# Masks of the attention maxima copied into PSUM by ScalarE instead of multiplied in by TensorE, with three rotating bank pairs and an earlier norm of the next input

## What is computed

```python
def xattn(query_in, ctx, mask, ...):            # both layers; mask and inner norms in the second only
    q = layernorm(query_in @ Wq + bq) ; k = layernorm(ctx @ Wk + bk) ; v = layernorm(ctx @ Wv + bv)
    scores = einsum('bhqd,bhkd->bhqk', heads(q), heads(k)) / sqrt(32)
    scores = where(mask == 0, -1e9, scores)      # mask: 2 x 2048 x 154, int32
    return merge(softmax(scores) @ heads(v)) @ Wo + bo
x = x + tanh(g_xattn[0]) * L0_xattn(layernorm(x), ctx)
x = x + tanh(g_ffn[0])   * L0_ffn(layernorm(x))          # 512 -> 2048 -> 512, relu
x = x + tanh(g_xattn[1]) * L1_xattn(ctx, layernorm(x), mask)
x = x + tanh(g_ffn[1])   * L1_ffn(layernorm(x))          # piecewise-linear gelu on a fixed-point grid
```

## Time and profile before

| | us |
|---|---|
| median of 3 runs | 2468.31 |
| lowest, highest | 2467.7, 2469.46 |
| the profiled execution | 2469.93 |
| its span in the profile | 2468.1 |
| TensorE busy | 2407.3 (98%) |
| TensorE weight loads busy | 1826.9 (74%) |
| VectorE busy | 1444.4 (59%) |
| ScalarE busy | 1086.7 (44%) |
| GpSimd busy | 244.6 (10%) |

### The profile page before, as it was taken

One profiled execution on the slowest core, in us unless ns is written; L12 is line 12 of the kernel. 1 busy time (PEld: TensorE's weight loads), 2 busy tenths in 40 slices (PEclk: granted clock), 3 DMA queues, 4 the chain that ended last, 5 costly groups with the idle time before them and its releaser, 6 DMA issues.

```text
span 2468.1 us, 33136 instructions
## 1 busy us (share of the span) xinstructions
PE 2407.3 (98%) x13344; PEld 1826.9 (74%) x13344; DVE 1444.4 (59%) x2410; ACT 1086.7 (44%) x1762; POOL 244.6 (10%) x223
## 2 busy tenths in 40 slices
PE   6999999999999999999989999999999999999998
PEld 5666667688888888888755666666778888888886
DVE  5555566542212222223566666665888888888986
ACT  4343433442222222223344333335566666666665
POOL 1011112210000000000311111113000000000000
PEclk9999999999999999999999999999999999999999
DMA  3121111421101101102311222223401101001000
GB/s 126 35 86 52 52 52 69 157 87 52 42 11 52 52 14 38 52 18 72 124 61 62 79 78 79 79 73 114 156 18 35 52 18 52 35 25 45 35 32 21
DMA packets 92600, 147.27 MB, mean 60 GB/s; under 512 B 5408, under 2 KB 28320, under 8 KB 92448
## 3 DMA queue, kind: packets, MB, share of 16 engines
q1 hardware_dynamic: 92448, 145.16, 17.6%
HBM read 111.59 MB, written 33.55 MB: 59 GB/s over the span
## 4 chain that ended last, share of the span: by engine, by line
PE 39%; DVE 9%; ACT 2%; issue 1%; DMA 0%; POOL 0%; SPq 0%; DVEq 0%; ACTq 0%
PE l_lay_bank L69 18%; PE l_lay_score L69 11%; PE l_lay_score L1416 1%; PE l_lay_score L1418 1%; PE l_lay_values L1494 1%; PE l_lay_sums L1506 1%; PE l_lay_values L1498 1%; DVE l_at_at_next L1036 1%; DVE l_at_h_lo L1050 1%; DVE l_at_at_next L1029 1%; PE l_lay_score L1477 1%; DVE l_at_full L1025 1%; DVE l_at_full L1018 1%; DVE l_at_xTf_lo L924 1%; DVE l_at_lay_stats L891 1%
## 5 line engine op out<-in xcount | busy, mean ns | idle before, releaser
L69 PE MATMUL l_lay_score<-l_at_tw_hi,l_at_h_hi 128*128 128x512 f32 x1024 | 401.5, 392 | 5.2 <-DVE l_at_h_lo L1050 4.7
L69 PE MATMUL l_lay_bank<-l_at_xTf_hi,l_at_tw_hi 128*128 128x512 f32 x1024 | 400.0, 391 | 0.0
L69 PE MATMUL l_lay_score<-l_at_tw_hi,l_at_h_lo 128*128 128x512 f32 x1024 | 398.7, 389 | 0.0
L69 PE MATMUL l_lay_score<-l_at_tw_lo,l_at_h_hi 128*128 128x512 f32 x1024 | 398.5, 389 | 0.0
L69 PE MATMUL l_lay_bank<-l_at_xTf_hi,l_at_tw_lo 128*128 128x512 f32 x1024 | 398.5, 389 | 0.0
L69 PE MATMUL l_lay_bank<-l_at_xTf_lo,l_at_tw_hi 128*128 128x512 f32 x1024 | 398.4, 389 | 0.0
L1010 DVE TENSOR_TENSOR l_at_h_lo<-l_at_full,l_at_h_hi 128x512 fp32r<-128x512 f32 x128 | 99.6, 779 | 465.9 <-ACT l_at_h_hi L740 465.9
L735 ACT ACTIVATE l_at_full<-l_lay_bank,l_at_lay_b 128x512 f32<-128x512 f32 x128 | 88.3, 690 | 457.6 <-PE l_lay_bank L69 457.6
L69 PEld LDWEIGHTS l_lay_score<-l_at_tw_hi,l_at_h_hi 128*128 128x128 f32 x1024 | 192.3, 188 | 49.2 <-DVE l_at_h_lo L1050 10.2
L69 PEld LDWEIGHTS l_lay_score<-l_at_tw_hi,l_at_h_lo 128*128 128x128 f32 x1024 | 192.2, 188 | 40.2
L69 PEld LDWEIGHTS l_lay_bank<-l_at_xTf_hi,l_at_tw_lo 128*128 128x128 f32 x1024 | 192.2, 188 | 40.0
(11 more groups left out here) (224 smaller groups left out, 4071.9 us busy)
## 6 DMA issues: line engine op xcount, KB each, us to landing
both_x_in<-stream SPq DMA_DIRECT2D x25, 1024.0 KB, 5.6
l_at_xg<-stream SPq DMA_DIRECT2D x23, 1024.0 KB, 5.6
stream<-l_at_xg SPq DMA_DIRECT2D x22, 1024.0 KB, 4.3
l_at_tw_raw<-in_l_w SPq DMA_DIRECT2D x64, 256.0 KB, 5.7
l_at_maskT_in<-in_maskT SPq DMA_DIRECT2D x40, 256.0 KB, 2.7
both_x_in<-in_x SPq DMA_DIRECT2D x9, 1024.0 KB, 7.6
l_at_xg<-in_x SPq DMA_DIRECT2D x7, 1024.0 KB, 5.4
out<-l_at_xg SPq DMA_DIRECT2D x7, 1024.0 KB, 4.3
```

Of the source, the lines that this page charges most:

```text
L69: done = nc.tensor.matmul(out, lhs[a], rhs[b], start=first and n == 0, stop=last and n == len(passes) - 1)
```

## The change

In the second layer, for chunks 1 to 7 and maxima 4 to 15, the mask is no longer multiplied in. ScalarE copies `mask_add` into the two banks (`seed_max`), and the key products accumulate onto it (start is false). The maxima 4 to 15 rotate over three bank pairs, the third being `values` and `sums`, now banks 4 and 5 of one tensor of six. A seed waits for the maximum three before it, seed 4 for the masks and for ScalarE's own copies of values and sums. TensorE waits for the seed instead of for the maximum two before. The high halves of query tiles 2 and 3 are made behind seeds 5 and 6. On VectorE, in the second layer, mask, first mask piece and the statistics of the next input stand behind the second query row, and its normalisation behind the third; GpSimd makes the input's scale before the queries' one.

```diff
-        score = n.ps("score", [P, GH, 512])
-        values = n.ps("values", [P, 512])
-        sums = n.ps("sums", [P, 512])
+        score = n.ps("score", [P, GH + 2, 512])
+        values, sums = score[:, GH, :], score[:, GH + 1, :]
...
+        SEED0 = 4
+        N_SEED = NM - SEED0
+        pair_of = lambda it, m: m % 2 if it == 0 or m < SEED0 else (m - 2) % 3
+        pair_before = lambda m: m - 3 if m > SEED0 else None
+        max_banks = lambda it, m: score[:, 2 * pair_of(it, m):2 * pair_of(it, m) + 2, 0:2 * KEYS]
...
+            def seed_max(it, m):
+                if m == SEED0:
+                    act.wait_ge(mask_done, it + 1)
+                    act.wait_ge(c_out, KT * it)
+                    act.wait_ge(s_out, it)
+                else:
+                    act.wait_ge(max_done, NM * it + pair_before(m) + 1)
+                nc.scalar.activation(max_banks(it, m).rearrange("p a (h k) -> p a h k", h=2),
+                                     mask_add[:, m % QT, :].unsqueeze(1).unsqueeze(1)
+                                     .broadcast_to([P, 2, 2, KEYS]), ACT.Copy).then_inc(seeded, 1)
...
                 c_evict(it, 3)
                 if more and norm:
-                    q_front_norm(it + 1, (2, 3))
+                    q_raw_norm(it + 1, 2)
+                    q_raw_norm(it + 1, 3)
                 s_evict(it)
+                if more and norm:
+                    for m in range(SEED0, NM):
+                        seed_max(it + 1, m)
+                        if m in (SEED0 + 1, SEED0 + 2):
+                            q_hi_norm(it + 1, m - SEED0 + 1)
...
+                    q_rows_front(it + 1, (0, 1))
+                    mask_front(it + 1)
+                    maskT_front(it + 1, 0)
+                    norm_stats(it + 2)
+                    q_rows_front(it + 1, (2,))
+                    norm_apply(it + 2)
+                    q_rows_front(it + 1, (3,))
                     q_norm_stats(it + 1)
+                    q_norm_apply(it + 1)
...
             def max_of(it, m):
                 t, q, b = m // QT, m % QT, it // CPB
+                seed = norm and it > 0 and m >= SEED0
...
-                if m >= 2:
+                if seed:
+                    pe.wait_ge(seeded, N_SEED * (it - 1) + m - SEED0 + 1)
+                elif m >= 2:
                     pe.wait_ge(max_done, NM * it + m - 1)
...
-                    if norm:
+                    if norm and not seed:
                         nc.tensor.matmul(to, ident_bf[:, :], mask_add[:, q, :].unsqueeze(1)
                                          .broadcast_to([P, 2, KEYS]), start=True, stop=False)
```

More of the change, by code:

```diff
@@ L590, in _ @@
                     add_bias(last, gate_bias)
+                if it < last:
+                    x_rstd_of(it + 2)
                 if norm and it < last:
                     q_rstd_of(it + 1)
-                if it < last:
-                    x_rstd_of(it + 2)
                 if it:
@@ L1189, in _ @@
                     k_lo_of(1)
-                for half in ((0, 1), (2, 3)):
-                    if norm:
-                        q_rows_front(it + 1, half)
-                    else:
-                        q_front(it + 1, half)
-                    if not norm and half[0] == 0:
-                        norm_stats(it + 2)
-                if norm:
+                if norm:
+                    q_rows_front(it + 1, (0, 1))
[5 more added lines that the diff above has]
+                    q_rows_front(it + 1, (3,))
                     q_norm_stats(it + 1)
-                    norm_stats(it + 2)
                     q_norm_apply(it + 1)
                 else:
+                    q_front(it + 1, (0, 1))
+                    norm_stats(it + 2)
+                    q_front(it + 1, (2, 3))
                     norm_apply(it + 2)
@@ L1419, in max_of @@
                                             keys.bd[:, b, t, 2 * a:2 * a + 2, :],
-                                            start=not norm, stop=True)
+                                            start=not norm, stop=True, skip_group_check=seed)
                 done.then_inc(max_ps, 1)
```

27 lines of the change are left out of this document (13 added, 14 removed).

## The result

The changed kernel takes 2473.65 us (median of 10 runs, 2470.68 to 2475.73), beside 2468.51 for the kernel before, timed anew with it (10 runs, 2467.11 to 2469.46): a ratio of 1.002, 95% interval 1.0012 to 1.0028. That is 5.1 us slower, where 3.0 were forecast. Its profiled execution took 2475.56 us with a span of 2473.8, against 2469.93 and 2468.1.

What follows compares the result with a forecast made beforehand. TensorE was taken to bound six of the seven loops, VectorE the first. Six loops at 0.0, six earlier starts -0.5 and first loop +3.5 gave +3.0: 2472.9 profiled, 2471.3 us median, range 2459 to 2481.

Steps and rivals of the forecast that it cites:

- Removed, 3.4 us a loop: TensorE, second layer: two mask products fewer for each of 12 maxima save 3.4 us a loop, 24 in all.
- The seed, 0.71: ScalarE: each added 128x616 copy of the mask into PSUM takes 0.71 us, starting every 0.63.
- The chain: High half, low half, maximum and seed run serially; VectorE waits 2.1 and 1.4 us, TensorE 1.4 and 1.7.
- Steady loops, 0.0: The six loops after the first: the waits use up what the removed mask products free, gain 0.0 us.
- The early norm, -0.5: VectorE's earlier mask and normalisation shorten one TensorE wait of 0.47 us by 0.08 in six chunks: -0.5 us.
- The first loop, +3.5: First of seven loops, bound by VectorE: removed columns give nothing, the serial waits cost in full, +3.5 us.
- The clock: TensorE's granted clock was expected not to fall, the forecast waits being no longer than those in a window at 1.00.
- My rival: TensorE at half its pace for 10 us in each loop: +35 us, 2503; chance 0.03.
- four links in seven loops: Each 0.1 us of a seed counts four times in a loop, about 0.4 us in each of seven loops.
- the first rival: TensorE keeps its pace because ScalarE's high halves come before VectorE asks: 2447, half of it 2459; chance 0.17.
- The chain does not bind: ScalarE's high halves are out before VectorE asks, six loops gain up to 20.5 + 0.5 us: 2447; chance 0.17.
- The seed is dear: Seeds 4 to 7 of each loop cost 1.0 us each: +11.6, 2479.9; chance 0.25.

Runs made afterwards that it cites:

- version with unused products: Changed kernel plus three products nobody reads on TensorE ahead of each wait for a seed in the first loop: 2472.13 us.
- version with late low halves and unused products: Changed kernel with VectorE's low halves 2 and 3 behind maxima 5 and 6, plus two unread products before each first-loop seed wait: 2452.71 us.
- seeds only: Changed kernel with the reorder of VectorE and GpSimd undone, seeds and three bank pairs kept: 2474.6 us.
- the repaired one: Changed kernel with VectorE's low halves of query tiles 2 and 3 moved behind maxima 5 and 6: 2452.66 us.
- a dearer seed: Changed kernel with each seed made as two copies of 308 elements a row, one for each bank: 2473.91 us.
- the version with the first loop as before: Changed kernel, first loop with mask products, two bank pairs and low halves behind maxima 2 and 3; later loops' low halves behind 5 and 6: 2452.03 us.
- late low halves: Changed kernel with VectorE's low halves of query tiles 2 and 3 behind maxima 5 and 6 instead of 2 and 3: 2452.66 us.
- before, first unmasked: Kernel before without the mask products of maxima 4 to 15 in the first of the seven loops: 2469.33 us.

## Why the prediction was nearly right

The sign, the range and the main mechanism came as forecast; the size was 2.3 us low, and that by two errors that partly cancel, so that it came so near is in part luck. Step by step, against the profiled executions (+3.0 forecast, +5.7 measured):

- *Removed, 3.4 us a loop.* Right: with the chain cut 2.8 of it arrive, and 0.6 go to VectorE's low halves.
- *The seed, 0.71.* 0.688 measured. The estimate of 0.70 from the Trainium skill's page "ScalarE: Activation LUTs" (What ACT_TABLE_LOAD costs) agrees; its tip on placement, by which I would have gone to 0.6 and a sum near 0, doesn't show here beyond the 0.025 us between 0.688 and the 0.713 of the earlier trace rows.
- *The chain.* Waits of VectorE of 2.13 and 1.30 (2.1 and 1.4 forecast), of TensorE 1.01 and 1.45 (1.4 and 1.7). Counted from the transposes before, maximum 7 starts at 1490.07 on the clock of the kernel before (1497.04 less 1446.48 - 1439.51), where I had 1490.2. The rate is right too: 0.09 us of seed gave 0.37 a loop.
- *Steady loops, 0.0.* They are 0.3 shorter: 0.13 from that start, 0.14 from my allowance of 0.4 for weights and late seeds, of which 0.26 were needed (10.95 from maximum 7 to the transposes, 10.69 without it).
- *The early norm, -0.5.* Nothing; TensorE's wait went from 0.47 to 0.44, not by 0.08. Together with the steady loops the six later loops give -1.64 without the clock (from the version with unused products: 63.02, 61.54, 61.52, 61.49, 61.50, 61.50), where -0.5 stood.
- *The first loop, +3.5.* +3.66. VectorE's two waits are there as forecast (2.13 and 1.30 us); some 0.4 of it may be the clock (by the version with late low halves and unused products), and then the chain is 3.3. It is not measured in this kernel, and a fall 3 us longer cost its first loop nothing (seeds only).
- *The clock.* This step failed: "the waits I forecast are no longer than those in that window". By the lengths of single waits it was nearly true: TensorE's longest wait in that window is not among the, it is the one of 1.57 us behind the end of the loop, at a clock of 1.00, and I had forecast 1.4 and 1.7 for the steady loops. But the first loop has no output products between its maxima, and by the times of my own chain its waits are over 2 us (2.16 and 2.16 came); I had not written them down. And the comparison was the wrong one: I had read that the clock stayed at 1.00, not what kept it there, four products a maximum in a loop that VectorE sets. With two of the four gone it fell behind waits of at most 0.8 us. The falls cost 3.8 us in the second and third loop. The Trainium skill's page "TensorE: Matmul & The Clock Gate" (Part 1), which I had dismissed by that comparison, says that TensorE is taken to half its clock after being idle. The traces agree that idle time is what brings 0.50, but it came without an idle stretch of over 0.8 us, behind 5.40 us with 2.72 busy. My rival held the mechanism with a price of +35 for every loop and a chance of 0.03; it came at a tenth of the price, in three loops.
- *The bounds.* By my own rate of four links in seven loops a seed of 1.0 us gives 0.29 x 28 = 8.1 and so +11.1, not +11.6, and half of the first rival is 2458, not 2459. Nothing measured hangs on either.

So +3.66 - 1.64 + 3.76 = +5.8. Without the falls the changed kernel would have been near 2470, and my number 1.4 too high instead of 2.3 too low. "The chain does not bind", 2447, was far off for this kernel and near for the repaired one (2452). "The seed is dear" fell at 0.69.

What stays open: what decides where the clock falls. Neither the length of a wait nor the busy time just ahead settles it: in a steady loop of the changed kernel TensorE was busy 2.95 of the 5.40 us up to 1497.04 and kept 1.00, and in the version with the first loop as before it was busy 3.74 of the 5.40 us up to 1304.10, where the clock fell. So it is open why the last four loops keep the full clock through the same two waits; why in the second loop it fell in two kernels and not in the one with a dearer seed, whose waits are longer; and in which loops it fell in the runs without a profile.

## What to carry to other kernels

When work moves from a busy engine to a third one, write down the in-order queue of every engine around it: two copies placed behind refills that wait for VectorE cost 2.5 us in each loop, and moving their consumers three places on VectorE gave it back. Before columns are taken off TensorE, look where another engine sets its pace: there they cost nothing and may be what holds its clock, as in the first loop here. A chain of waits can be priced from the rows of before, to 0.1 us here, but the clock can't be forecast from the length of one wait (1.57 us at 1.00 before, a fall with no wait over 0.8 in another kernel). When idle time is added to TensorE, take a fall in that loop and the next ones as a rival with a price from rows at the lower level, some us here.

## What the runs showed of the hardware

- ScalarE fills 616 fp32 columns of two PSUM banks from a bf16 row in 0.688 us, next to 0.713 us for a copy of 616 within SBUF (of 32 partitions); a copy of 308 columns takes 0.415.
- TensorE's granted clock fell to half among waits of 1.35 to 2.16 us, but also with no wait over 0.8, when only the columns of the loop were fewer; it stayed at 1.00 through a single wait of 1.57 and through waits of 1.45 in four loops.
- What a fall costs depends on the loop: 2.46 us for some 7 us at half and 1.30 for some 3 us where TensorE sets the pace, about 0.4 for some 10 us (late low halves) and some 7 us (before, first unmasked) where VectorE does, and nothing for the first 3 us of the second loop.
- In the kernel with the seed in two copies one of the steady loops, the sixth, had a clock of 0.97 and took 1.35 us more, with the code and the waits of its neighbours. Why it fell there is not shown. Single runs of one kernel differ in their mean granted clock in the same way (0.990 to 0.995, and 2478 to 2469.5 us, with unused products), so a profile with one such loop isn't read as the effect of an edit.
